# A fused eight-layer kernel: every fourth value-key product of the third layer's scan moves from VectorE to GpSimd

## The reference: what is computed

```python
q = silu(x @ wq); k = x @ wk; v = x @ wv            # [b, n, 16 heads, 8]
z = cumlogsumexp(concat([0, k]))                     # per channel, over time
log_f = z[:-1] - z[1:];  k = exp(k - z[1:])
q = concat([q * cos, q * sin]);  k = concat([k * cos, k * sin])   # 16 features a head
def step(S, (qt, kt, vt, lt)):
    S = exp(lt)[..., None] * S + kt[..., None] * vt[..., None, :]   # [features, 8]
    o = einsum('bhe,bhev->bhv', qt, S)
```

## Time and profile before

| what | value |
|---|---|
| median of 3 runs | 1271.48 us (1271.02 to 1272.04) |
| the profiled execution, its time | 1269.26 us |
| its span in the trace | 1267.4 us |
| mean granted TensorE clock | 0.912 of full speed |
| busy, share of the span: PE | 968.5 us, 76% |
| DVE | 947.0 us, 75% |
| ACT | 634.4 us, 50% |
| POOL | 632.4 us, 50% |

### The profile page before, as it was taken

One profiled execution on the slowest core, in us unless ns is written; L12 is line 12 of the kernel. 1 busy time (PEld: TensorE's weight loads), 2 busy tenths in 40 slices (PEclk: granted clock), 3 DMA queues, 4 the chain that ended last, 5 costly groups with the idle time before them and its releaser, 6 DMA issues.

```text
span 1267.4 us, 12569 instructions
## 1 busy us (share of the span) xinstructions
PE 968.5 (76%) x3012; PEld 551.5 (44%) x3012; DVE 947.0 (75%) x1236; ACT 634.4 (50%) x1155; POOL 632.4 (50%) x452
## 2 busy tenths in 40 slices
PE   5307988668878996389999999876767666675896
PEld 2103333223324653278888888532222222223684
DVE  4995787799987647656666666587999999965564
ACT  4424475600026466156555565777455555553455
POOL 3721054746651014167777777502666666613572
PEclk9758999779998998699999999987899999996998
DMA  2000110000002000176666666200000000000661
GB/s 71 0 0 1 53 58 15 1 0 0 1 0 71 1 16 7 37 157 145 144 157 152 142 146 149 60 1 0 1 0 0 0 0 0 1 13 11 152 151 34
DMA packets 18639, 61.62 MB, mean 49 GB/s; under 512 B 2560, under 2 KB 12416, under 8 KB 12800
## 3 DMA queue, kind: packets, MB, share of 16 engines
q1 hardware_dynamic: 18608, 61.26, 20.6%
HBM read 59.54 MB, written 1.70 MB: 48 GB/s over the span
## 4 chain that ended last, share of the span: by engine, by line
PE 45%; DVE 35%; issue 7%; ACT 5%; POOL 4%; DMA 2%; DVEq 1%; SPq 0%; POOLq 0%; ACTq 0%
PE ps L346 44%; DVE g L1352 5%; DVE g L1155 5%; DVE tmp L1155 4%; DVE y L1602 3%; ACT rstd L735 2%; ACT g L735 2%; POOL g L1142 2%; DVE g L1602 2%; DVE parts L1291 2%; DVE parts L1155 2%; DVE resid L1155 2%; DVE g L1559 1%; DMA g<-coef_scratch 1%; POOL sq L1038 1%
## 5 line engine op out<-in xcount | busy, mean ns | idle before, releaser
L346 PE MATMUL ps<-parts 128*128 128x512 f32 x1800 | 450.0, 408 | 32.6 <-DVE parts L1155 9.7
L346 PEld LDWEIGHTS ps<-parts 128*128 128x128 f32 x1800 | 345.4, 195 | 136.5 <-DVE parts L1155 18.0
L735 ACT ACTIVATE g<-ps 128x512 f32<-128x512 f32 (+3 forms) x322 | 189.9, 597 | 327.1 <-PE ps L346 297.2
L1085 POOL TENSOR_TENSOR parts<-g,parts 128x512 fp32r<-128x512 f32 x168 | 217.6, 1295 | 155.5 <-ACT parts L735 151.5
L346 PE MATMUL ps<-g,arena 128*128 128x512 f32 (+1 forms) x304 | 152.5, 644 | 93.0 <-DVE g L1155 42.5
L1142 POOL TENSOR_TENSOR g<-g 128x1024 f32<-128x1024 f32 x64 | 150.2, 2352 | 132.6 <-ACT g L735 130.9
L1155 DVE TENSOR_TENSOR ps<-g,ps 128x512 f32<-128x512 f32 x168 | 116.9, 696 | 112.5 <-PE ps L346 90.7
L735 ACT ACTIVATE parts<-g 128x512 fp32r<-128x512 f32 (+2 forms) x252 | 126.3, 534 | 30.3 <-DVE g L1451 15.9
L346 PEld LDWEIGHTS ps<-g,arena 128*128 128x128 f32 (+1 forms) x304 | 57.4, 201 | 187.6 <-issue 66.7
L1038 POOL TENSOR_TENSOR sq<-resid 128x512 f32<-128x512 f32 x32 | 35.9, 1122 | 199.0 <-DVE resid L1155 184.7
L1155 DVE TENSOR_TENSOR g<-ps,g 128x512 f32<-128x512 f32 x160 | 110.7, 692 | 32.1 <-DMA g<-coef_scratch 14.2
(11 more groups left out here) (168 smaller groups left out, 1107.2 us busy)
## 6 DMA issues: line engine op xcount, KB each, us to landing
g<-coef_scratch SPq DMA_DIRECT2D x80, 512.0 KB, 6.2
g<-in_moe_dram SPq DMA_DIRECT2D x42, 192.0 KB, 4.8
g<-in_rope_dram SPq DMA_DIRECT2D x1, 2048.0 KB, 9.0
arena<-in_weights_dram SPq DMA_DIRECT2D x1, 1348.5 KB, 5.8
sel<-in_selectors_dram SPq DMA_DIRECT2D x1, 1152.0 KB, 7.2
arena<-in_weights_dram SPq DMA_DIRECT2D x1, 1028.5 KB, 4.9
g<-in_x_dram SPq DMA_DIRECT2D x4, 256.0 KB, 3.8
out_dram<-g SPq DMA_DIRECT2D x4, 256.0 KB, 2.5
```

Of the source, the lines that this page charges most:

```text
L346: return nc.tensor.matmul(o, lhsT, rhs, start=start, stop=stop, **kw)
L735: return nc.scalar.activation(o, i, func, **kw)
L1085: pv.tensor_tensor(hid_lo[:, cols(c)], g[:, 6, (c % 2) * N:(c % 2 + 1) * N], hid_hi[:, cols(c)].bitcast(F32), ALU.subtract).then_inc(s["hl ...
```

## The change

`inputs(k)` for every k with k % 4 == 3 (8 of the 32 steps) is no longer done by DVE. ACT copies the value bank of such a step to one of two halves of `sq` (`v_copy(k)`, semaphore `v_copied`), and POOL multiplies this copy by the two rows of key features into the same buffer `two_of(0, 11, k)` (`features_in(k)`, semaphore `in_pool`). POOL does `features_in(3)` ahead of its first query product, and `features_in(k + 4)` right behind the query product of step k, for each k with k % 4 == 3. The bank is free for PE when ACT has copied it. DVE's last wait before the scans becomes a semaphore of its own, `kr_ready`, for which POOL waits too. PE's order is left as it is.

```diff
+        def of_pool(k):
+            return (k + 1) // 4
+        def of_dve(k):
+            return k + 1 - of_pool(k)
+        def v_copy(k):
+            return sq[:, k // 4 % 2 * N:(k // 4 % 2 + 1) * N]
...
                 if k >= 3:
-                    pe.wait_ge(s["vb_used"], k - 2)
+                    if (k - 3) % 4 == 3:
+                        pe.wait_ge(s["v_copied"], of_pool(k - 3))
+                    else:
+                        pe.wait_ge(s["vb_used"], of_dve(k - 3))
                 mm(ps[:, v_bank(k), :], W(2, "wv", e * 128, e * 128 + 128), H(c)).then_inc(s["vb_bank"], 1)
...
+            for k in range(3, 8 * CHUNKS, 4):
+                act.wait_ge(s["vb_bank"], k + 1)
+                if of_pool(k) > 2:
+                    act.wait_ge(s["in_pool"], of_pool(k) - 2)
+                f(v_copy(k), ps[:, v_bank(k), :], ACT.Copy).then_inc(s["v_copied"], 1)
             square("rms", lambda c: G(4, c), "og_ready", 0)
...
                     pool.wait_ge(s["qr_ready"], CHUNKS)
+                    def features_in(k):
+                        pool.wait_ge(s["v_copied"], of_pool(k))
+                        pv.tensor_tensor(two_of(0, 11, k), g[:, 6:8, cols(k // 8)],
+                                         v_copy(k).unsqueeze(1).to_broadcast([P, 2, N]), ALU.mult)\
+                            .then_inc(s["in_pool"], 1)
+                    pool.wait_ge(s["kr_ready"], 1)
+                    features_in(3)
                     for c in range(CHUNKS):
                         for e in range(8):
...
                                 fast_states(e), g[:, 8:10, cols(c)], ALU.mult).then_inc(s["qm_ready"], 1)
+                            k = 8 * c + e + 4
+                            if k % 4 == 3 and k < 8 * CHUNKS:
+                                features_in(k)
...
-                chain(tt(G(7, c), G(4, c), G(11, c)))
-            chain.wait()
+                last = tt(G(7, c), G(4, c), G(11, c))
+                if c + 1 < CHUNKS:
+                    chain(last)
+            last.then_inc(s["kr_ready"], 1)
+            dve.wait_ge(s["kr_ready"], 1)
...
-                if k + 1 < 8 * CHUNKS:
+                if k + 1 < 8 * CHUNKS and (k + 1) % 4 != 3:
                     inputs(k + 1)
                 e, c = k % 8, k // 8
-                dve.wait_ge(s["vb_used"], k + 1)
+                if k % 4 == 3:
+                    dve.wait_ge(s["in_pool"], of_pool(k))
+                else:
+                    dve.wait_ge(s["vb_used"], of_dve(k))
```

More of the change, by code:

```diff
@@ L149, in sandwich @@
             q_bank2 k_bank2 g1_bank g2_bank k2_ready sigq_ready q_used g1_ready gate_ready
-            m_ready md_ready me_ready s_ready rs_ready vb_bank vb_used st_ready
+            m_ready md_ready me_ready s_ready rs_ready vb_bank vb_used v_copied in_pool kr_ready st_ready
             qm_ready qm_used og_ready nrm_ready wo_bank setup2
```

## The result

| | median | lowest to highest | runs |
|---|---|---|---|
| before | 1271.3 us | 1270.94 to 1272.96 | 6 |
| changed | 1310.99 us | 1309.65 to 1312.86 | 6 |

The ratio is 1.0311, 95% interval 1.0298 to 1.0324: the change costs 39.7 us. The profiled execution of the changed kernel took 1312.77 us, with a span of 1311.0 us, 43.6 us above the span of before. 3.8 us more lie behind it, nearly all of them in the seventh layer's scan, which the change does not touch: over the same 200 us of the program the mean clock is 0.94, and was 0.97 in the profiled execution of before.

What follows compares the result with a forecast made beforehand. DVE bound the kernel before; the new loop would set the pace. Loops and start +25.8 us, clock +13.3, together 39.1 on a median of 1271.5, gave 1310.5 us; range 1294 to 1318.

Steps and rivals of the forecast that it cites:

- What bounds the scan before: DVE sets the pace of the third layer's scan at 3.49 us a step: 2.37 for two scans, 1.12 for its product.
- The prices: Added work in the scan: eight ACT copies at 597 ns each and eight new POOL products at 2.36 us each.
- The dearer product: POOL's new product slowed beside DVE's scans, 4.1 us in place of 2.36; kept for the range only.
- The wait: POOL idle before seven of eight new products, for head sums, value matmul and ACT's copy: 3.63 us each.
- The loop: Scan, four steps: from one query product through PE, ACT, POOL and DVE to the fourth after, 17.3 us, before 13.9.
- The start: Scan's beginning, POOL doing features_in(3) first: query product of step 3 ends at 278.6, not 276.12, 2.5 us late.
- The clock: PE's pauses of about 5.5 us drop its clock to half: 1.9 us in each of seven loops, 13.3 us.
- the one on the other side: Rival: DVE stays the scan's bound and the 9 us are won, 1262.5 us; chance 0.04.
- The threshold: POOL's wait at the new product: under 1.0 us DVE's 12.8 paces four steps; at 2.1 us the 13.9 of before.

Runs made afterwards that it cites:

- the control: The kernel before with the value matmuls one step earlier on PE and nothing moved to POOL or ACT: 1271.18 us, ratio 0.9994.
- e4_both: The changed kernel with each new product one query product later on POOL and the value matmuls one step earlier on PE: 1262.01 us, ratio 0.9926.
- the filled kernel: The changed kernel with five extra matmuls adding zeros in each of PE's seven long pauses: 1296.41 us, ratio 1.0196.
- e2_values_first: The changed kernel with the value matmuls one step earlier on PE, POOL's order kept: 1276.43 us, ratio 1.0033.
- e1_product_later: The changed kernel with each new product one query product later on POOL, behind that of step k - 3: 1269.95 us, ratio 0.9988.
- the run with every third step: The kernel of e4_both with every third step from 5 to 29 on POOL, nine products, none at the start: 1260.35 us, ratio 0.9917.
- the run with every fourth step: The kernel of e4_both, both orders changed against the changed kernel, every fourth step on POOL: 1262.01 us, and 1262.05 us when run again.

## Why the prediction was right

Forecast 1310.5 us, measured 1310.99. Point by point:

- **What bounds the scan before.** DVE, at 3.49 us a step. Shown by the control (a better order on PE alone wins nothing) and by `e4_both` (the removed products come out as 12.79 us for four steps).
- **The prices.** The copy 0.60 us as taken, the new product 2.34 in place of 2.36; DVE's scans did not slow it. The dearer product that the range allowed for is ruled out in this kernel.
- **The wait.** 3.63 us worked out, 3.61 measured, at all seven places.
- **The loop.** 17.3 us for four steps worked out, 17.20 measured with the clock held (new products from 282.44 to 385.62, six turns). With the clock held the stretch from the first DVE product to the last query product takes 137.6 us (259.61 to 397.21) against 113.7 before: 23.9 us for loop and start, where the forecast had 25.8. 1.1 of the 1.9 us too much lie in the start.
- **The start.** The query product of step 3 was to end at 278.6; it ended at 278.37, the low clock included, which the forecast had put into this term.
- **The clock.** This was the term with the least under it, 1.9 us a turn. Measured: new products start at 281.99 and 398.12, six turns, 19.36 us each, less 17.20 with the clock held, so 2.16 us on average, under the bound of 2.6. Over the whole stretch the clock cost 15.8 us (153.4 less 137.6), start and last turn included, where the forecast had 13.3; by the times of whole executions it is the 14.6 us above, since the filled kernel's scan begins 1.2 us later. The mean clock of the stretch was to be near 0.8 and is 0.85. The rule of the Trainium skill (TensorE: Matmul & The Clock Gate, "HAM oscillation — how this bites in real kernels"), that bursts parted by waits start cold each time, holds here in every turn of the changed kernel, as the windows and the head sums of 3.43 to 3.78 us above show.

The loop with its start was put 1.9 us too high and the clock 2.5 us too low; the two cancel, and a hit within half a microsecond is partly luck. The range and the mechanism do not hang on it. From the first DVE product to the last query product I gave about 153 us, and it is 153.4. DVE's idle time before its products in the scan was to be some 45 us, and is 43.1.

Of the rivals, the one on the other side named its point of decision well: whether the value matmul of step k + 4 runs before the head sums of step k. `e2_values_first` did exactly this and left a wait of 1.64 us, under the 2.1 at which the rival has the time of before; but the time was 4 to 5 us above before, not under it. The threshold was reckoned without the clock, and as such it holds: where the clock stays at 1.00, four steps take 13.4 us, which is POOL's 11.8 and the wait of 1.64. What it leaves out is that the pauses of PE that remain (2.8 us) still meet the low clock in some turns; 6.5 of the 8.6 us that DVE waits for PE in that run lie in the three turns at the start and with a fall.

## What to carry to other kernels

Before work is moved to an engine with room, list what the receiving engine does just before it, and follow what the moved work's input waits for: if the chain leads back to that very instruction, the free share of the engine is worth nothing, and each instance costs its wait and what stands behind it (a wait of 3.61 us cost 5 to 6 us here). One place later in the queue was worth 3% here. If such a round trip makes TensorE pause (2.1 to 5.4 us in these runs), look at the clock behind the pause, since half speed may then fall on just those matmuls on which everybody waits.

## What the runs showed of the hardware that was not expected

**A pause of 2.84 us does not decide the clock.** `e2_values_first` has six pauses of 2.83 to 2.85 us in front of head sums. Behind four of them the head sums have records of 1.98 us, behind two 3.47 and 3.78. `e1_product_later` has a fall as well behind a pause of 2.05 us (the matmuls at 299.29, 3.65 us). The two pauses in the trace of before, 7.01 and 3.48 us, had shown no such short case. What tells the turns apart was not tried.

**Longer records without a lower rate.** GpSimd's products, at 2341 to 2360 ns in all kernels with some slack, averaged 2398 ns (x9) and 2392 ns (x32) in the run with every third step, where GpSimd and VectorE are both busy without a break:
```profile
L1158 POOL TENSOR_TENSOR g<-g 128x1024 f32<-128x1024 f32 x32 | 75.0, 2392 | 16.6 <-DVE g L1392 16.6
...
L1147 POOL TENSOR_TENSOR g<-g,sq 128x1024 f32<-128x1024 f32 x9 | 21.6, 2398 | 0.0
```
This looks like contention, but the starts say otherwise:
```profile
307.07 2.42 POOL L1158 TENSOR_TENSOR g<-g 128x1024 f32<-128x1024 f32 x1
...
309.38 2.42 POOL L1147 TENSOR_TENSOR g<-g,sq 128x1024 f32<-128x1024 f32 x1
```
They lie 2.31 us apart, as they do on average over 32 products of this run (272.45 to 346.35), and in the run with every fourth step two products back to back start 2.31 us apart too (315.87 and 318.18). The longer records overlap the next one, and the rate is the same. What the extra length is stays open.
